# The second head's q and k as plain products, and new orders for the front, in a pre-norm attention and FFN kernel

## The chip, the cores and the metric

One Trainium2 chip, one core. The metric is the device time of one execution in microseconds (us). All inputs lie in the chip's memory when it starts and the output is written back to it.

## The reference

`x` is 1024 tokens by 512. Attention has 32 heads of width 128 (each head's q takes 192 columns of `wq`, of which the first 128 are used), then an FFN of three layers whose weights are signs.

```python
h = layernorm(x)
q = h @ wq  -> [S, 32, 192]; q = q[..., :128]
k, v = h @ wkv[:, :4096], h @ wkv[:, 4096:8192]   # [S, 32, 128] each
scores = q k^T / sqrt(192), causal mask, softmax over keys
x = x + (probs @ v) @ wo
h = layernorm(x)
x = x + ei(relu(ei(relu(s0 * h @ sign(k0)) * 2, k1, s1)) * 2, k2, s2)
```

`ei` multiplies the last fifth of its input by -4 before the product with +1 and -1 weights. The normalisations have no gain or bias.

## The kernel before, in words

Precision comes from pairs: every operand is held as a high and a low half (f16, or f32r for the output projection and the FFN), and a product is three matmuls, high by high, high by low, low by high. `xb` holds the normalised input, transposed, in blocks; `wqk` the halves of a head's q and k weights in slots A11, A12, S1 to S4 and A22.

**Heads.** From the second head on, q and k of a head come from seven products (steps `x1` to `x7`, `product`, L1138; six matmuls of 128x512 each). They are a Strassen-like scheme over 2 by 2 blocks: sums of weight blocks (`sums`, L508, on GpSimd), sums T1 to T4 of input blocks (`block_sum` and the split `sum_lo_part`, L872, on VectorE, with `sum_hi_part`, L646, on ScalarE), and gathers (`a2` to `a7`, `gather`, L878) that add the results into `qk32`. ScalarE and GpSimd split those into halves (`qk`). The first head has plain products instead (steps `y0` to `y3`, `plain_product`, L1150; twelve matmuls of 128x512 each), whose results go straight into `qkT`: high half on ScalarE (`plain_product_hi`, L657), low half on VectorE (L901). 

**Steps of a head.** `s0` to `s7` are scores of 128 queries against all earlier keys, into one of two PSUM buffers by turns; `m` the mask and maxima (VectorE), `e` the exponentials (ScalarE), `h` and `l` the high and low halves of the probabilities (ScalarE, VectorE, into four buffers of `p16`), `t` a transposing DMA of them (issued by SyncE). s(n) waits for l(n-2); h(n) waits for the t of four steps before, which frees its buffer. `v` projects values for a pair of heads, `pv` multiplies probabilities by values, `o` projects the output, with its addition on VectorE under the same name.

**Weights.** A head's q and k weights are loaded (`lqk`), their squares summed on ScalarE (`mx`), the 128 partial sums written to memory and read back spread over all partitions (`put`, `get`, both issued by SyncE; for the first weights a transpose on TensorE, `spread`, does this), a power-of-two scale is found (`sc`, `bounds`, VectorE), the weights scaled (`r`, ScalarE), and split on GpSimd (`wqk` for q, `wk` for the first head's k; `wv` for values, `wo` for the output).

**Order.** Each engine runs an order written out by hand for a group of two heads (L40 to L73), one string for the steady group and one for the front, in words such as `x3@2`: step x3 of the head that is 2 after the group's first. The front is group -1, so `@2` there is the first head, `@3` the second and `@4` the third. Groups -1, 0 and the last are written out in code and the rest is a loop (`groups`, L358). Each engine does its steps strictly in this order, SyncE too: a DMA behind a waiting one waits with it. The front also normalises the second half of the input (`stat`, `scale`, `root`, `apply`, `turn`, `nhi`, `nlo`, `keep`). Chains of matmuls use four PSUM banks; a chain waits until the one before it in its bank has been read (`bank_free`, L1120), in the front round robin, later by the string BANKS. `exists` (L95) drops what a head does not need; `wait` (L340) turns a head's count into a semaphore value.

Of the kernel before, what the change touches and what calls it, by code (L numbers as in the profile page):

```python
# [35 lines left out]

PLAIN = (Q0, K0, Q1, K1)
# [6 lines left out]
    spread2@2 y0@2 y1@2 turn4@2 turn5@2 turn6@2 turn7@2 v0@2 s0@2 v1@2 s1@2 v2@2 v3@2 y2@2 s2@2 y3@2 s3@2 x1@3 v4@2  # L44
    s4@2 x2@3 v5@2 s5@2 x3@3 v6@2 s6@2 v7@2 s7@2""", "")
# [23 lines left out]
    lqk0@4 lo0@2 t0@2 put0@4 get0@4 t1@2 t2@2 t3@2 t4@2""", "")  # L69
# [3 lines left out]
    wqk0@2 wk0@2 wv0@2 wv1@2 wqk0@3 sum0@3""", "")  # L73
# [21 lines left out]
def exists(g, step):  # L95

    h = GH * g + step[1]
    if h == 0 and (step[0] in ("x", "a", "snap", "sum", "qk", "mx", "sc", "r", "put", "get", "lqk", "lv") or step[0] == "wv" and step[2] == 2):
# [100 lines left out]
def build(nc, hidden, wq, wkv, wo, k0, s0, k1, s1, k2, s2, out):  # L199
# [21 lines left out]
    with ExitStack() as ctx:  # L221
# [118 lines left out]
        def wait(eng, s, g, per, j, n):  # L340

            if isinstance(g, int):
                if per * (GH * g + j) + n > 0:
                    eng.wait_ge(s, per * (GH * g + j) + n)
            else:
                assert per * (GH + j) + n > 0
                eng.wait_ge(s, g * (GH * per) + (per * j + n))

        def wait_pair(eng, s, g, per, j, n):

            if isinstance(g, int):
                if per * (g + j // GH) + n > 0:
                    eng.wait_ge(s, per * (g + j // GH) + n)
            else:
                assert per * (1 + j // GH) + n > 0
# [60 lines left out]
        def loading_step(q, g, step, j, n):  # L416

            if step == "lqk":
                wait(q, sum_lo, g, 3, j, -6)
                if isinstance(g, int) and GH * g + j == 2:  # L420
                    q.wait_ge(first_lo, 1)
                    q.wait_ge(plain_lo, 1)
                load_head(q, g * GH + j, j % 2)
            elif step == "lo":
                wait(q, wo_lo, g, 1, j, 0)
                load_out(q, g * GH + j)
            elif step == "lv":
                wait_pair(q, wv_lo, g, 3, j, -1)
                load_values(q, g + j // GH)
            elif step == "put":  # L430
                rows_to_dram(q, g, j, n)
            elif step == "get":
                rows_from_dram(q, g, j, n)

        @block.sync
        def _(sp):
# [15 lines left out]
            def sync_steps(g):  # L452
                for step, j, n in steps_of(SYNC_ORDERS, g):
                    if step == "t":
                        wait(sp, p_lo, g, 8, j, n + 1)
                        sp.sem_inc(turn_go, 1)
                        if isinstance(g, int) and GH * g + j == 1 and n == 0:
                            sp.wait_ge(t_lo, 4)


                        sp.dma_start_transpose(pT[:, j % 2, rows_of(n), :], p16[:, n % 4, 0:2 * (n + 1) * P]) \
                            .then_inc(turned[n % 4], 16)
                    else:
# [17 lines left out]
        def _(pool):  # L481
# [11 lines left out]
            def split_first(g, j):  # L493

                wait(pool, scaled[0], g, 1, j, 1)
                if isinstance(g, int) and GH * g + j == 1:
                    pool.wait_ge(plain_done, 3)
                wait(pool, done["x"], g, 7, j, -5 - 7)
                split(raw[:, j % 2 * 2, :], slots(HI, A11, 2), slots(LO, A11, 2), first_hi, first_lo,
                      lambda: wait(pool, first_hi, g, 1, j, 1), not (isinstance(g, int) and GH * g + j == 0))  # L500

            def split_plain():

                pool.wait_ge(plain_hi, 1)
                nc.gpsimd.tensor_tensor(slots(LO, S2, 2), raw[:, 1, :], slots(HI, S2, 2), ALU.subtract) \
                    .then_inc(plain_lo, 1)

            def sums(g, j):  # L508
# [17 lines left out]
                split(k, slots(HI, S1, 2), slots(LO, S1, 2), sum_hi, sum_lo,
                      lambda: wait(pool, sum_hi, g, 3, j, 2 - 3))
                wait(pool, sum_done, g, 4, j, 4 - 4)
                split(q, slots(HI, S3, 2), slots(LO, S3, 2), sum_hi, sum_lo,
                      lambda: wait(pool, sum_hi, g, 3, j, 3 - 3))  # L530

            def qk_lo(g, j, n):
                wait(pool, qk_hi_done[n], g, 1, j, 1)
                wait(pool, gathered[LAST[n]], g, 1, j, 0)
# [54 lines left out]
            def pool_steps(g):  # L589
                for step, j, n in steps_of(POOL_ORDERS, g):  # L590
                    if step == "wqk":
                        split_first(g, j)
                    elif step == "wk":
                        split_plain()
# [27 lines left out]
        def _(act):  # L622
# [29 lines left out]
            def keep_x1(g, j, bank):  # L652
                wait(act, done["x"], g, 7, j, 1 - 7)
                wait(act, gathered[3], g, 1, j, -1)
                nc.scalar.activation(x1[:, :], psC[:, bank, :], ACT.Copy, scale=OUT_DOWN).then_inc(x1_kept, 1)

            def plain_product_hi(n, bank):  # L657
                act.wait_ge(plain_done, n + 1)
                nc.scalar.activation(qkT[:, qk_slot(0, PLAIN[n]), HI, :], psC[:, bank, :], ACT.Copy, scale=OUT_DOWN) \
                    .then_inc(qk_hi_done[PLAIN[n]], 1)  # L660

# [144 lines left out]
        def _(dve):  # L806
# [17 lines left out]
            def norm_scale(b):  # L824
# [5 lines left out]
                dve.wait_ge(mv_done, 4 * b + 4)  # L830
                ve, root, inv, a, bb = (nrm[:, k, :] for k in range(5))
                nc.vector.tensor_scalar_add(ve, mv[:, first:first + 4, 1], EPS).then_inc(ve_done, 1)
# [45 lines left out]
            def gather(g, j, n, bank):  # L878

                wait(dve, done["x"], g, 7, j, n - 7)  # L880
                if n < 4:
                    wait(dve, x1_kept, g, 1, j, 0)
# [4 lines left out]
                for earlier in {4: (3,), 5: (4,), 6: (5,), 7: (5,)}.get(n, ()):  # L887
                    wait(dve, gathered[earlier], g, 1, j, 0)
# [12 lines left out]
            def plain_product_lo(n, bank):  # L901
                hi, lo = (qkT[:, qk_slot(0, PLAIN[n]), w, :] for w in (HI, LO))
                dve.wait_ge(qk_hi_done[PLAIN[n]], 1)
                nc.vector.scalar_tensor_tensor(lo, psC[:, bank, :], OUT_DOWN, hi, ALU.mult, ALU.subtract) \
                    .then_inc(qk_lo_done[PLAIN[n]], 1)
# [79 lines left out]
            def vector_step(g, step, j, n):  # L985
                if step == "stat":
                    norm_stats(n)
                elif step == "scale":
                    norm_scale(n)
                elif step == "apply":  # L990
# [33 lines left out]
            norm_scale(0)  # L1024
            for t in range(4):
# [29 lines left out]
            norm_scale(2)  # L1055
            for t in range(4):
# [7 lines left out]
            norm_scale(3)  # L1064
            ffn_lo(0)
# [20 lines left out]
        def _(pe):  # L1086
# [33 lines left out]
            def bank_free(g, before):  # L1120

                if before is None:
                    return
                kind, j, n = before
                if kind == "x":
                    wait(pe, x1_kept if n == 1 else gathered[n], g, 1, j, 0)
                elif kind == "y":
                    pe.wait_ge(qk_lo_done[PLAIN[n]], 1)
# [7 lines left out]
            def product(g, j, n, bank):  # L1136
# [4 lines left out]
                elif n == 3:  # L1141
                    wait(pe, sum_lo, g, 3, j, 0)
                if isinstance(g, int) and GH * g + j == 1 and b in T_USED:
# [6 lines left out]
            def plain_product(n, bank):  # L1150

                if n == 0:
                    pe.wait_ge(first_lo, 1)
                elif n == 1:
                    pe.wait_ge(plain_lo, 1)
                c, a = n // 2, (A11, S2)[n % 2]
# [27 lines left out]
            def project_v(g, j, n, bank):  # L1184

                if isinstance(g, int) and g + j // GH == 0:
                    if n == 0:
                        pe.wait_ge(bounded[0], 6)
# [41 lines left out]
            def tensor_step(g, step, j, n):  # L1230
# [6 lines left out]
                else:  # L1237
                    at = PLAN[(g if isinstance(g, int) else 1), step, j, n]
                    bank_free(g, at[1])
# [19 lines left out]
            spread(1)  # L1259
# [6 lines left out]
            def ffn_chain(k):  # L1266
# [10 lines left out]
                if before[0] != "ffn":  # L1277
                    bank_free(NG, before)
# [54 lines left out]
```

## Time and profile before

| | |
|---|---|
| median of 3 runs | 1162.95 us (1162.06 to 1163.11) |
| the profiled execution | 1162.55 us, span 1160.7 us |
| TensorE matmul busy | 1102.2 us, 95% |
| VectorE, ScalarE, GpSimd busy | 899.0, 678.8, 676.9 us |
| chain that ended last | TensorE 66%, VectorE 14%, issue 9%, ScalarE 6% |
| 40 to 90 us: mean granted clock in steps of 10 us | 1.00, 0.83, 0.66, 0.77, 0.72 |

The page has shares of the whole span; a timeline gives one engine's instructions with the idle time ahead of each and what ended it; a window gives busy time and granted clock of a stretch. PE is TensorE, PEld its weight loads, DVE VectorE, ACT ScalarE, POOL GpSimd, SPq SyncE's DMA issues. L numbers are lines of the kernel.

### The profile page before, as it was taken

The page shows a single profiled execution, that of the slowest core. Times are in us where ns is not written, and L with a number is a line of the kernel's source. Part 1 is how long each engine was busy: PE and PEld are TensorE (multiplying, and loading weights), DVE is VectorE, ACT ScalarE, POOL GpSimd, SP SyncE. Part 2 cuts the span into 40 slices and gives each one's busy share as a digit, 9 for nine tenths or more (in the row PEclk, how much of TensorE's full clock was granted, in tenths as well). Part 3 has the DMA queues.
Part 4 walks back from the last instruction along what each step waited for, and adds up shares of the span by engine and source line. Part 5 has one row for each costly group of instructions (what it writes and reads, how often), then busy time and mean ns, then how long its engine had stood idle before and what let it go on. Part 6 is the DMA issues. An engine that isn't in the chain of part 4 may idle for free.

```text
span 1160.7 us, 22159 instructions
## 1 busy us (share of the span) xinstructions
PE 1102.2 (95%) x6217; PEld 655.3 (56%) x6217; DVE 899.0 (77%) x1799; ACT 678.8 (58%) x1335; POOL 676.9 (58%) x694
## 2 busy tenths in 40 slices
PE   4859999999999999999999999999999999999898
PEld 2515555556565555556555555656565555656577
DVE  6658777887878777787878787787877787787873
ACT  6545665656565565666565565566665565655453
POOL 2417576675656667665657657665657757665300
PEclk9979999999999999999999999999999999999999
DMA  4055664545554553555554553555454554555601
GB/s 154 4 118 90 112 104 89 114 104 118 111 122 83 123 104 75 124 105 122 111 111 81 119 114 73 120 115 124 97 116 87 109 113 85 118 99 99 105 1 73
DMA packets 367511, 117.33 MB, mean 101 GB/s; under 512 B 313088, under 2 KB 361344, under 8 KB 367488
## 3 DMA queue, kind: packets, MB, share of 16 engines
q1 hardware_dynamic: 367488, 117.05, 48.1%
q8 instruction: 11, 0.18, 0.1%
q14 instruction: 12, 0.10, 0.0%
HBM read 39.39 MB, written 2.12 MB: 36 GB/s over the span
## 4 chain that ended last, share of the span: by engine, by line
PE 66%; DVE 14%; issue 9%; ACT 6%; POOL 3%; DMA 1%; DVEq 1%; ACTq 0%; SPq 0%; POOLq 0%
PE psC L1094 38%; PE psS L1094 14%; PE psC L1218 13%; DVE p L966 3%; DVE attn L949 2%; ACT attn L725 2%; DVE qk L899 2%; ACT raw L671 1%; DVE psS L959 1%; POOL wqk L488 1%; DVE res L982 1%; ACT psS L703 1%; POOL wqk L485 1%; DMA wmax_rows<-wmax 1%; DVE bound L921 1%
## 5 line engine op out<-in xcount | busy, mean ns | idle before, releaser
L1094 PE MATMUL psC<-xb,wqk 128*128 128x512 f16 x1350 | 331.9, 385 | 18.6 <-POOL wqk L488 8.0
L703 ACT ACTIVATE psS<-psS,negmax 128x128 f32<-128x128 f32 (+7 forms) x256 | 182.8, 714 | 238.1 <-DVE negmax L959 235.9
L1094 PE MATMUL psC<-wos,attn 128*128 128x512 f32 x768 | 254.3, 442 | 12.5 <-DVE attn L949 8.9
L959 DVE CUSTOM_DVE_ANT_0 psS<-psS,mask,undo_qk 128x128 f32<-128x128 f32 (+7 forms) x256 | 209.2, 822 | 67.9 <-PE psS L1094 50.8
L966 DVE SCALAR_TENSOR_TENSOR p<-psS,p 128x128 f16<-128x128 f32 (+7 forms) x256 | 193.0, 754 | 72.8 <-ACT p L711 69.8
L1094 PE MATMUL psS<-qkT 128*128 128x512 f16 (+3 forms) x1152 | 231.4, 328 | 6.9 <-DVE p L966 4.8
L1094 PEld LDWEIGHTS psC<-xb,wqk 128*128 128x128 f16 x1350 | 124.6, 99 | 169.9 <-issue 26.3
L982 DVE SCALAR_TENSOR_TENSOR res<-psC,rinv,res 128x512 f32<-128x512 f32 x256 | 190.4, 744 | 11.2 <-DVE rinv L973 6.9
L1218 PE MATMUL psC<-pT,v 128*128 128x512 f16 (+3 forms) x1152 | 197.6, 326 | 0.2 <-DMA pT<-p 0.2
L536 POOL TENSOR_TENSOR qkT<-qk,qkT 128x512 f16<-128x512 f32 x124 | 141.5, 1157 | 92.7 <-ACT qkT L696 89.6
L1094 PE MATMUL psC<-wvs,xb 128*128 128x256 f16 x1536 | 189.0, 273 | 0.5 <-issue 0.4
L711 ACT ACTIVATE p<-psS 128x128 f16<-128x128 f32 (+7 forms) x256 | 166.2, 649 | 20.4 <-DMA pT<-p 2.7
L485 POOL TENSOR_TENSOR wqk<-raw,one 128x512 f16<-128x512 f32 x124 | 115.7, 933 | 100.8 <-ACT raw L671 90.1
L1094 PEld LDWEIGHTS psC<-wos,attn 128*128 128x128 f32 x768 | 137.2, 190 | 63.3 <-DVE attn L949 16.1
L1094 PEld LDWEIGHTS psC<-wvs,xb 128*128 128x128 f16 x1536 | 147.3, 98 | 39.0 <-issue 12.5
L1218 PEld LDWEIGHTS psC<-pT,v 128*128 128x128 f16 x1152 | 108.8, 98 | 92.4 <-issue 5.2
L1094 PEld LDWEIGHTS psS<-qkT 128*128 128x128 f16 x1152 | 98.1, 98 | 109.5 <-issue 38.0
L488 POOL TENSOR_TENSOR wqk<-raw,wqk 128x512 f16<-128x512 f32 (+1 forms) x125 | 130.6, 1045 | 16.3 <-ACT wqk L690 6.5
L485 POOL TENSOR_TENSOR wvs<-raw,one 128x512 f16<-128x512 f32 x45 | 46.8, 1039 | 113.8 <-ACT raw L671 80.2
L899 DVE SCALAR_TENSOR_TENSOR qk<-psC,qk 128x512 f32<-128x512 f32 x124 | 98.8, 817 | 12.3 <-PE psC L1094 10.5
L696 ACT ACTIVATE qkT<-qk 128x512 f16<-128x512 f32 x124 | 75.9, 624 | 41.3 <-DVE qk L899 41.3
L717 ACT ACTIVATE v<-psC 128x256 f16<-128x256 f32 x128 | 48.7, 381 | 58.9 <-PE psC L1094 58.9
(90 smaller groups left out, 934.0 us busy)
## 6 DMA issues: line engine op xcount, KB each, us to landing
raw<-in_L_attn_wkv SPq DMA_DIRECT2D x64, 256.0 KB, 3.3
raw<-in_L_attn_wq SPq DMA_DIRECT2D x32, 256.0 KB, 3.4
raw<-in_L_attn_wo SPq DMA_DIRECT2D x32, 256.0 KB, 3.2
pT<-p SPq DMA_TRANSPOSE x256, 4.3
wrow<-wmax_rows SPq DMA_DIRECT2D x45, 64.0 KB, 4.6
res<-in_L_attn_hidden_states SPq DMA_DIRECT2D x8, 256.0 KB, 5.6
out<-res SPq DMA_DIRECT2D x8, 256.0 KB, 2.0
raw<-in_L_ffn_k SPq DMA_DIRECT2D x3, 256.0 KB, 3.9
```

Source lines behind the costliest of these rows:

```text
L485: nc.gpsimd.tensor_tensor(hi, src, one[:, :].to_broadcast([P, src.shape[1]]), ALU.mult) \
L488: nc.gpsimd.tensor_tensor(lo, src, hi, ALU.subtract).then_inc(lo_sem, 1)
L536: nc.gpsimd.tensor_tensor(lo, qk32[:, AT[n], :], hi, ALU.subtract) \
L696: nc.scalar.activation(qkT[:, qk_slot(j, n), HI, :], qk32[:, AT[n], :], ACT.Copy) \
L703: nc.scalar.activation(row, row, ACT.Exp, bias=negmax[:, n:n + 1], scale=-1.0, accum_out=rowsum[:, j % 2, n:n + 1]) \
L711: nc.scalar.activation(parts_of(n)[:, :, HI, :], psS[:, n % 2, 0:(n + 1) * P].rearrange("p (k s) -> p k s", s=P), ACT.Copy, scale=UP).then ...
L899: nc.vector.scalar_tensor_tensor(to, product, OUT_DOWN, base32, ALU.mult, ALU.add).then_inc(gathered[n], 1)
L959: nc.vector.tensor_tensor_reduce(row, row, mask[:, S - width:S], undo_qk[:, j % 2:j % 2 + 1], 3e38, ALU.add, ALU.min, negmax[:, n:n + 1]). ...
L966: nc.vector.scalar_tensor_tensor(parts[:, :, LO, :], psS[:, n % 2, 0:(n + 1) * P].rearrange("p (k s) -> p k s", s=P), UP, parts[:, :, HI, ...
L982: nc.vector.scalar_tensor_tensor(res[:, t, :], psC[:, bank, :], rinv[:, t:t + 1], res[:, t, :], ALU.mult, ALU.add).then_inc(added, 1)
L1094: last = nc.tensor.matmul(out_ap, w, x, start=k == 0, stop=k == len(terms) - 1)
L1218: last = nc.tensor.matmul(o, a, b, start=(kt == 0 and k == 0), stop=(kt == count - 1 and k == 2))
```

## The change

The second head's q and k are plain products too (`y4` to `y7`: q and k of tokens 0 to 511, then of 512 to 1023). Its q weights go to S3 and S4, its k weights to A11 and A12. Seven products, six gathers, GpSimd's sums and splits of that head are gone, and T1 to T4 are first read by the third head. All semaphore counts follow, a second group is written out ahead of the loop, `norm_scale` is cut in two with the part behind the square root in `norm_rest`, `spread1` moves behind `y0`, and the orders of the front are new on all five engines.

```diff
-    spread2@2 y0@2 y1@2 turn4@2 turn5@2 turn6@2 turn7@2 v0@2 s0@2 v1@2 s1@2 v2@2 v3@2 y2@2 s2@2 y3@2 s3@2 x1@3 v4@2
-    s4@2 x2@3 v5@2 s5@2 x3@3 v6@2 s6@2 v7@2 s7@2""", "")
+    y0@2 spread1@2 y1@2 spread2@2 turn4@2 turn5@2 turn6@2 turn7@2 v0@2 v1@2 v2@2 s0@2 s1@2 y2@2 s2@2 s3@2 y3@2 v3@2
+    s4@2 v4@2 s5@2 y4@2 v5@2 s6@2 y5@2 s7@2 y6@2 v6@2 y7@2 v7@2""", "")
...
-    nhi0@2 nhi1@2 mx1@2 nhi2@2 nhi3@2 mx0@3 keep0@2 keep1@2 keep2@2 keep3@2 r1@2 root1@2 r0@3 y0@2 vhi0@2 vhi1@2
-    y1@2 nhi4@2 nhi5@2 nhi6@2 nhi7@2 keep4@2 keep5@2 keep6@2 keep7@2 v0@2 e0@2 h0@2 v1@2 e1@2 h1@2 v2@2 v3@2 y2@2
-    e2@2 h2@2 y3@2 part0@2 e3@2 h3@2 mx0@4 part1@2 snap0@3 v4@2 e4@2 h4@2 v5@2 e5@2 h5@2 part2@2 v6@2 part3@2 e6@2
-    h6@2 v7@2 r0@4 e7@2 h7@2""", "")
+    nhi0@2 nhi1@2 nhi2@2 keep0@2 nhi3@2 mx0@3 keep1@2 keep2@2 mx1@2 keep3@2 root1@2 r1@2 vhi0@2 vhi1@2 nhi4@2 nhi5@2
+    y0@2 nhi6@2 keep4@2 keep5@2 nhi7@2 v0@2 keep6@2 y1@2 keep7@2 mx0@4 e0@2 h0@2 e1@2 h1@2 v1@2 v2@2 y2@2 e2@2 h2@2
+    e3@2 y3@2 r0@3 h3@2 part0@2 part1@2 e4@2 h4@2 v3@2 v4@2 e5@2 y4@2 h5@2 part2@2 part3@2 v5@2 y5@2 e6@2 h6@2 e7@2
+    h7@2 y6@2 r0@4 v6@2 y7@2 v7@2""", "")
...
-    nlo0@2 nlo1@2 nlo2@2 nlo3@2 sc1@2 sc0@3 stat4@2 stat5@2 stat6@2 stat7@2 scale1@2 apply4@2 apply5@2 apply6@2
-    apply7@2 y0@2 y1@2 nlo4@2 nlo5@2 nlo6@2 nlo7@2 v0@2 m0@2 sum0@2 l0@2 v1@2 m1@2 sum1@2 l1@2 v2@2 v3@2 y2@2 m2@2
-    l2@2 y3@2 part0@2 m3@2 l3@2 part1@2 v4@2 m4@2 l4@2 a2@3 sum2@2 v5@2 m5@2 l5@2 sum3@2 part2@2 v6@2 m6@2 l6@2
-    part3@2 a3@3 v7@2 m7@2 sc0@4 l7@2""", "")
+    nlo0@2 nlo1@2 nlo2@2 nlo3@2 stat4@2 stat5@2 stat6@2 stat7@2 scale1@2 sc1@2 rest1@2 apply4@2 apply5@2 apply6@2
+    apply7@2 nlo4@2 nlo5@2 sc0@3 nlo6@2 y0@2 nlo7@2 y1@2 v0@2 m0@2 m1@2 l0@2 sum0@2 l1@2 sum1@2 m2@2 m3@2 v1@2 l2@2
+    y2@2 v2@2 y3@2 sum2@2 l3@2 m4@2 part0@2 m5@2 l4@2 v3@2 sum3@2 v4@2 l5@2 m6@2 y4@2 part1@2 m7@2 v5@2 l6@2 sc0@4
+    y5@2 part2@2 l7@2 v6@2 y6@2 v7@2 part3@2 y7@2""", "")
...
-    lqk0@4 lo0@2 t0@2 put0@4 get0@4 t1@2 t2@2 t3@2 t4@2""", "")
+    lqk0@4 lo0@2 put0@4 t0@2 t1@2 get0@4 t2@2 t3@2 t4@2""", "")
...
-    wqk0@2 wk0@2 wv0@2 wv1@2 wqk0@3 sum0@3""", "")
+    wqk0@2 wk0@2 wv0@2 wv1@2 wqk0@3 wk0@3""", "")
...
+    if h <= 1 and step[0] in ("x", "a", "snap", "sum", "qk", "wqk"):
+        return False
...
             body(-1)
             body(0)
-            with eng.Fori(1, NG - 1) as g:
+            body(1)
+            with eng.Fori(2, NG - 1) as g:
...
-                wait(q, sum_lo, g, 3, j, -6)
-                if isinstance(g, int) and GH * g + j == 2:
-                    q.wait_ge(first_lo, 1)
-                    q.wait_ge(plain_lo, 1)
+                wait(q, sum_lo, g, 3, j, -9)
+                if isinstance(g, int) and GH * g + j in (2, 3):
+                    q.wait_ge(first_lo, GH * g + j - 1)
+                    q.wait_ge(plain_lo, GH * g + j - 1)
...
+                if isinstance(g, int) and GH * g + j == 2:
+                    pool.wait_ge(plain_done, 8)
+                wait(pool, done["x"], g, 7, j, -5 - 14)
+                to = S3 if isinstance(g, int) and GH * g + j == 1 else A11
+                split(raw[:, j % 2 * 2, :], slots(HI, to, 2), slots(LO, to, 2), first_hi, first_lo,
+                      lambda: wait(pool, first_hi, g, 1, j, 1), not (isinstance(g, int) and GH * g + j == 0))
+
+            def split_plain(h):
+
+                to = (S2, A11)[h]
+                if h == 1:
                     pool.wait_ge(plain_done, 3)
+                split(raw[:, 2 * h + 1, :], slots(HI, to, 2), slots(LO, to, 2), plain_hi, plain_lo,
+                      lambda: pool.wait_ge(plain_hi, h + 1), h == 1)
...
+            def norm_rest(b):
+
+                first = 4 * (b % NC)
                 ve, root, inv, a, bb = (nrm[:, k, :] for k in range(5))
-                nc.vector.tensor_scalar_add(ve, mv[:, first:first + 4, 1], EPS).then_inc(ve_done, 1)
                 dve.wait_ge(root_done, b + 1)
                 link(nc.vector.reciprocal(inv, root))
...
-            spread(1)
             groups(pe, tensor_steps)
```

## Rows read from the trace of the kernel before

**Rows 1.** The page: busy us, share of the span, instructions; then 40 slices.

```profile
PE 1102.2 (95%) x6217; PEld 655.3 (56%) x6217; DVE 899.0 (77%) x1799; ACT 678.8 (58%) x1335; POOL 676.9 (58%) x694
...
PE   4859999999999999999999999999999999999898
...
PEclk9979999999999999999999999999999999999999
```

**Rows 2.** Windows: length, then busy us of PE, PEld, DVE, ACT, POOL; clock; DMA.

```profile
43.00:79.00 36.00, 22.70 (x105) 10.93 (x103) 21.07 (x35) 17.41 (x30) 9.30 (x9) 0.81 0.38 81
...
43.00:86.20 43.20, 27.82 (x117) 12.57 (x115) 24.05 (x38) 19.96 (x35) 12.86 (x13) 0.76 0.38 79
...
110.00:210.00 100.00, 98.46 (x566) 57.57 (x565) 79.71 (x157) 60.03 (x121) 63.55 (x64) 1.00 0.59 111
300.00:400.00 100.00, 98.55 (x566) 57.58 (x565) 79.68 (x157) 59.39 (x118) 66.86 (x67) 1.00 0.48 102
```

**Rows 3.** Timeline of PE: start us, us, instruction, idle before it and its releaser.

```profile
31.43 0.33 PE L1094 MATMUL psS<-qkT 128*128 128x128 f16 x3 [1.84 <-ACT pT L642]
...
38.93 2.75 PE L1094 MATMUL psC<-xb,wqk 128*128 128x512 f16 x12
...
46.88 1.47 PE L1094 MATMUL psC<-wvs,xb 128*128 128x256 f16 x12
...
51.84 2.72 PE L1094 MATMUL psC<-xb,wqk 128*128 128x512 f16 x6 [2.51 <-issue]
...
63.11 2.74 PE L1094 MATMUL psS<-qkT 128*128 128x512 f16 x6 [4.57 <-DVE p L966]
...
72.16 4.33 PE L1094 MATMUL psC<-xb,wqk 128*128 128x512 f16 x12 [3.71 <-DVE v L943]
80.79 5.13 PE L1094 MATMUL psC<-xb,wqk 128*128 128x512 f16 x12 [4.30 <-DVE qk L899]
86.25 0.33 PE L1094 MATMUL psS<-qkT 128*128 128x128 f16 x3 [0.34 <-issue]
```

**Rows 4.** Timeline of SyncE's issues of DMAs.

```profile
48.26 0.35 SPq L406 DMA_DIRECT2D wmax_rows<-wmax  x1
55.80 0.33 SPq L413 DMA_DIRECT2D wrow<-wmax_rows  x1
56.24 6.04 SPq L461 DMA_TRANSPOSE pT<-p  x4
```

**Rows 5.** Timeline of ACT.

```profile
28.90 2.39 ACT L642 ACTIVATE pT<-psS 128x512 f32<-128x512 f32 x4 [0.55 <-DVE xb L859]
...
31.58 1.28 ACT L703 ACT_TABLE_LOAD   x1
...
47.09 1.05 ACT L685 ACTIVATE squares<-raw 128x1024 f16<-128x1024 f32 x1
...
61.25 0.81 ACT L711 ACTIVATE p<-psS 128x768 f16<-128x768 f32 x1 [2.67 <-DMA pT<-p]
...
74.10 1.15 ACT L671 ACTIVATE raw<-raw,bound 128x1024 f32<-128x1024 f32 x1 [4.91 <-DVE bound L929]
```

**Rows 6.** Timeline of DVE.

```profile
24.25 2.76 DVE L847 TENSOR_SCALAR xn<-res,mv,nrm 128x512 f32<-128x512 f32 x4
...
32.21 1.22 DVE L869 TENSOR_TENSOR xn<-pT 128x1024 f32<-128x1024 f32 x1
...
39.27 0.69 DVE L904 SCALAR_TENSOR_TENSOR qkT<-psC,qkT 128x512 f16<-128x512 f32 x1 [2.31 <-ACT qkT L659]
...
49.21 1.52 DVE L876 TENSOR_TENSOR xb<-xn,xb 128x1024 f16<-128x1024 f32 x1 [1.29 <-ACT xb L650]
...
64.10 1.22 DVE L876 TENSOR_TENSOR xb<-pT,xb 128x1024 f16<-128x1024 f32 x1
```

**Rows 7.** Timeline of POOL.

```profile
49.73 2.01 POOL L488 TENSOR_TENSOR wqk<-raw,wqk 128x512 f16<-128x512 f32 x1
...
79.17 1.04 POOL L485 TENSOR_TENSOR wqk<-raw,one 128x512 f16<-128x512 f32 x1
80.28 1.16 POOL L488 TENSOR_TENSOR wqk<-raw,wqk 128x512 f16<-128x512 f32 x1
```

More of the change, by code:

```diff
@@ L97, in exists @@
     h = GH * g + step[1]
-    if h == 0 and (step[0] in ("x", "a", "snap", "sum", "qk", "mx", "sc", "r", "put", "get", "lqk", "lv") or step[0] == "wv" and step[2] == 2):
+    if h <= 1 and step[0] in ("x", "a", "snap", "sum", "qk", "wqk"):
+        return False
+    if h == 0 and (step[0] in ("mx", "sc", "r", "put", "get", "lqk", "lv") or step[0] == "wv" and step[2] == 2):
         return False
@@ L345, in wait @@
             else:
-                assert per * (GH + j) + n > 0
+                assert per * (2 * GH + j) + n > 0
                 eng.wait_ge(s, g * (GH * per) + (per * j + n))
@@ L593, in pool_steps @@
                     elif step == "wk":
-                        split_plain()
+                        split_plain(j - 2)
                     elif step == "sum":
@@ L652, in keep_x1 @@
             def keep_x1(g, j, bank):
-                wait(act, done["x"], g, 7, j, 1 - 7)
-                wait(act, gathered[3], g, 1, j, -1)
+                wait(act, done["x"], g, 7, j, 1 - 14)
+                wait(act, gathered[3], g, 1, j, -2)
                 nc.scalar.activation(x1[:, :], psC[:, bank, :], ACT.Copy, scale=OUT_DOWN).then_inc(x1_kept, 1)
             def plain_product_hi(n, bank):
+                h, to = n // 4, PLAIN[n % 4]
                 act.wait_ge(plain_done, n + 1)
-                nc.scalar.activation(qkT[:, qk_slot(0, PLAIN[n]), HI, :], psC[:, bank, :], ACT.Copy, scale=OUT_DOWN) \
-                    .then_inc(qk_hi_done[PLAIN[n]], 1)
+                if h == 1 and to != K0:
+                    act.wait_ge(done["s"], 4 if to == Q0 else 8)
+                nc.scalar.activation(qkT[:, qk_slot(h, to), HI, :], psC[:, bank, :], ACT.Copy, scale=OUT_DOWN) \
+                    .then_inc(qk_hi_done[to], 1)
             def scale_weights(g, j, n):
@@ L692, in qk_hi @@
             def qk_hi(g, j, n):
-                wait(act, gathered[LAST[n]], g, 1, j, 0)
+                wait(act, gathered[LAST[n]], g, 1, j, -1)
                 wait(act, done["s"], g, 8, j, {Q0: -4, Q1: 0, K0: -8, K1: 0}[n])
@@ L878, in gather @@
             def gather(g, j, n, bank):
-                wait(dve, done["x"], g, 7, j, n - 7)
+                wait(dve, done["x"], g, 7, j, n - 14)
                 if n < 4:
-                    wait(dve, x1_kept, g, 1, j, 0)
+                    wait(dve, x1_kept, g, 1, j, -1)
                 reused = {2: Q0, 3: Q1, 4: K0, 5: K1}.get(n)
@@ L887, in gather @@
                 for earlier in {4: (3,), 5: (4,), 6: (5,), 7: (5,)}.get(n, ()):
-                    wait(dve, gathered[earlier], g, 1, j, 0)
+                    wait(dve, gathered[earlier], g, 1, j, -1)
                 product = psC[:, bank, :]
@@ L989, in vector_step @@
                     norm_scale(n)
+                elif step == "rest":
+                    norm_rest(n)
                 elif step == "apply":
@@ L1024, in _ @@
             norm_scale(0)
+            norm_rest(0)
             for t in range(4):
@@ L1055, in _ @@
             norm_scale(2)
+            norm_rest(2)
             for t in range(4):
@@ L1064, in _ @@
             norm_scale(3)
+            norm_rest(3)
             ffn_lo(0)
@@ L1118, in spread, with bank_free @@
                                     ident[:, :]).then_inc(spread_done, 1)
-            def bank_free(g, before):
+            def bank_free(g, bank, before):
                 if before is None:
+                    if bank == 3:
+                        pe.wait_ge(bounded[0], 6)
+                        pe.wait_ge(bounded[1], 1)
                     return
@@ L1125, in bank_free @@
                 if kind == "x":
-                    wait(pe, x1_kept if n == 1 else gathered[n], g, 1, j, 0)
+                    wait(pe, x1_kept if n == 1 else gathered[n], g, 1, j, -1)
                 elif kind == "y":
-                    pe.wait_ge(qk_lo_done[PLAIN[n]], 1)
+                    pe.wait_ge(qk_lo_done[PLAIN[n % 4]], 1 + n // 4)
                 elif kind == "v":
@@ L1141, in product @@
                 elif n == 3:
-                    wait(pe, sum_lo, g, 3, j, 0)
-                if isinstance(g, int) and GH * g + j == 1 and b in T_USED:
+                    wait(pe, sum_lo, g, 3, j, -3)
+                if isinstance(g, int) and GH * g + j == 2 and b in T_USED:
                     pe.wait_ge(t_lo, T_USED[b])
@@ L1150, in plain_product @@
             def plain_product(n, bank):
[L1152 to L1156, printed above, removed]
+                h, c, a = n // 4, n // 2 % 2, ((A11, S2), (S3, A11))[n // 4][n % 2]
+                pe.wait_ge(plain_lo if n % 2 else first_lo, h + 1)
                 pe.wait_ge(xt_lo, 4 * c + 4)
@@ L1277, in ffn_chain @@
                 if before[0] != "ffn":
-                    bank_free(NG, before)
+                    bank_free(NG, bank, before)
                 else:
```

47 lines of the change are left out of this document (19 added, 28 removed).

## The prediction

> **What bounds the kernel now.** I read the page's shares first [rows 1]. TensorE is busy for 1102.2 of 1160.7 us, at the full granted clock nearly everywhere; the two weak places are the first slices and the third, 58 to 87 us, which has 5 tenths busy and a clock of 7 tenths (so 1.2 GHz for part of it). The end of the kernel shows nothing comparable. The windows say the same with numbers [rows 2]: 100 us in the middle of the loop hold 98.55 us of matmul, 100 us that begin at 110 hold 98.46, and the 43.2 us from 43.0 hold only 27.82, at a mean clock of 0.76. From about 110 us on the kernel is matmul end to end, so whatever is won ahead of it comes out at the end one for one, unless the second group gives it back.
>
> So the place to read is TensorE's order of time there [rows 3]. The words of the orders are matched to it by shape: twelve 128x512 matmuls are one plain product y, six are one product x, twelve 128x256 are one v. Four waits stand out: 2.51, 4.57, 3.71 and 4.30 us, together 15.1. The work between them runs at half speed: six matmuls take 2.74 us, where twelve took 2.75 at 38.93. The other engines' rows name what each wait is for.
> - 2.51 us before x3 of head 1. It waits for every split of head 1's sums on GpSimd; the last, L488 at 49.73, takes 2.01 us [rows 7], to 51.74.
> - 4.57 us before s7 (63.11). s7 wants l5, that wants h5 on ScalarE, and h5 sat until 61.25 for a transposing DMA [rows 5]. SyncE issued four of those only at 56.24, behind get0@4, and this waited for put0@4 to land [rows 4]: the put was issued at 48.26 and the get at 55.80. The put in turn wanted the squares mx0@4 of 47.09 [rows 5]. A tiny DMA for a head that is two heads away holds up the transposes of head 0.
> - 3.71 and 4.30 us before x5 and x7 of head 1: their banks come free only through v7 and the gathers on VectorE, which stand behind l7 in its order, and l7 is late through the same delay, and on ScalarE r0@4 (74.10, after 4.91 us idle) stands ahead of e7 [rows 5].
>
> **The change part by part.** I take as mark the first scores of head 1, s0@1, at 86.25 [rows 3]. Beyond it both kernels issue the same steps in the same steady orders.
>
> *Work to the mark.* Prices at full clock, start to start: a y 2.6 us (38.93 to the next start 41.52; the row says 2.75), an x half of it, 1.3; a v 1.3 (46.88 to 48.19); s4 to s7 read 9984 columns, at 512 in 0.216 us 4.2 us. Before, from 42.17 where x1 of head 1 starts, there were x1 to x7, v4 to v7, s4 to s7 and x1 of the third head: 9.1 + 5.2 + 4.2 + 1.3 = 19.8 us of work. They took 86.25 - 42.17 = 44.1 us, so 24.3 us went to waits and to the half clock. After, from s4: four y, four v, s4 to s7 and x1 of the third head, 10.4 + 5.2 + 4.2 + 1.3 = 21.1. The second head's plain products thus cost 1.3 us (48 matmuls for 42).
>
> *What goes.* Nothing before the mark reads the sums of head 1, T1 to T4 or a gather. With the sums goes the 2.51 us; with the gathers and their banks go 3.71 and 4.30. put0@4 now stands ahead of t0, and mx0@4 ahead of e0, so the get waits beside t0 and t1 rather than in front of them; t1 is no longer behind it, and 4.57 goes too. With the four waits gone there should be no reason for the low clock.
>
> *What is late next, up to s4.* spread1 moves behind y0 and the reciprocal chain is split off as norm_rest, with sc1@2 between. y0 ends near 21.0, spread1 21.3, sc1@2 22.2, the rest 1.0 more, so the first apply is about 23.2 against 24.25 before; four applies take 2.76 [rows 6], and the turns and splits end about 0.7 us sooner. The last keep ends at 30.6 (before 28.90 + 2.39 = 31.3 [rows 5]). Behind it ScalarE now has mx0@4 (1.05) and the table load (1.28), both in [rows 5], then e0 and h0 (0.7): 33.7. VectorE: l0 0.3, sum0 1.15 (1.22 less overlap [rows 6]), l1 0.35, 35.5. TensorE has no filler there: s3 waits for l1, 0.65, then y3 2.6, to 38.8, v3 to 40.1. The halves of y3 (0.6 and 0.69 [rows 6]), with y2 and v2 ahead of it on VectorE, are ready at 40.5, and s4 starts then. All of y0 to y3, v0 to v3 and s0 to s3 is done at that point, which before was so at 42.17.
>
> *From s4 to the mark.* 19.8 us of TensorE's work before x1 bring v7's end to 60.3. I checked each want of it against the other queues: s5 wants l3 (42.2, reached at 42.6); y4 wants q of head 1 in S3, r0@3 to 40.9 and two GpSimd splits of 1.04 and 1.16 [rows 7], 43.3 against 43.6; y5 wants k, 45.6 against 48.7; s6 wants l4 (46.1 against 47.5); s7 wants l5 (48.8 against 51.3); y6 and y7 want banks freed long before. x1 of the third head wants A11, which y7 reads last: GpSimd's split starts at 59.1, while v7 still runs 1.3 us, and takes 2.25, so x1 waits 1.1 us. The mark would be 60.3 + 1.1 + 1.3 = 62.7.
>
> *Allowance.* VectorE held 21.07 us of work in 43 to 79 [rows 2]. After, it loses from this m3 and three gathers and gains y4 to y7 (0.69 each [rows 6]), about 21 us in the 22.2 us from 40.5: it has no slack, and TensorE and ScalarE each add small waits. The margins above are 0.3 and 0.4 us in two places. From 0 (all covered) to 9 us (every one of the five m, e, h, l rounds late by a split part or sum, about 1.8 each, 1.05 on ScalarE and 0.7 over the cover on VectorE); I take 1.5, near the lower end, since the later margins are 1.4 to 3 us. Mark at 64.2.
>
> *The port.* The L876 of 49.21 took 1.52 us while GpSimd worked, those of 64.10 took 1.22 with it idle [rows 6], and the L488 beside the first took 2.01 against 1.16 at 80.28 [rows 7]. After, part3 stands behind v7 on VectorE, at about 61, just where GpSimd makes the low half for x1. The Trainium skill (GPSIMD Engine Reference, Specifications) says that GpSimd shares its interfaces to SBUF with VectorE, in contention with instructions that have two SBUF inputs, which L876 has; the trace agrees. By it x1 would come up to 0.85 us later, and the sum be 0.85 worse. By the row at 80.28 nothing is added. The allowance holds either.
>
> *Smaller edits.* The second group leaves the loop: unrolled code at 110:210 is as dense as the loop at 300:400 [rows 2], so 0, within 0.5 us either way for an instruction fetch or a loop's start. Semaphore counts (-14, -9, 1-8 and so on) only follow two heads without sums: 0; the bank waits are the same kind. The later put1@0, get1@0 and wv0@2 keep their distance from the mark.
>
> Sum: 86.25 - 64.2 = 22.0 us less. The profiled execution took 1162.55 us (span 1160.7 and 1.85 around it), 0.4 under the median of 1162.95. 1162.55 - 22.0 = 1140.5 us.
>
> **Rivals.**
> *Half the gain.* One in-order queue falls behind: a 1.05-us part on ScalarE ahead of e4, e5 and e6 delays the round of scores, l and the next s. For it: VectorE has no slack, so a late l isn't made up. Against: y and v cover up to 3.9 us between scores. Five late rounds cost 9 us: 1149.5; three, 1146.
> *Slower, by the clock.* If the wait ahead of s3 and y3, about 1 us in my walk, grows to the 2.5 us of the row at 51.84, the clock falls there as it did in that row, and TensorE works from 36 us on at 1.2 GHz. y3, v3 and 21.1 us take double, 25 us more: 1165.5, slower than before. Against: the wait of 1.84 us before s0 of head 0 (31.43 [rows 3]) left the clock high, and my walk has half of that. It decides from about 2 us of wait on.
> *Given back.* The second group's own roundtrips (put1@0, get1@0) or GpSimd's sums of the third head set its start, and the mark moves without the rest: about 1161. Against: the puts follow mx1@2 at 62.8, as close to the mark as before, and the sums end at about 73 where x3 wants them at 81.
> *More than the sum.* The allowance isn't needed and the stall before the first o0 of head 0 shrinks: 1137.5.
>
> **How the numbers follow.** The sum 0.62; half the gain 0.22 (mostly 1144 to 1150); more than the sum 0.08; slower by the clock 0.04; given back 0.04. A run here can't tell under 0.2% (2.3 us) from nothing, so same is most of the given-back case, 0.03; slower 0.04; faster 0.93. The likeliest case alone spans 1137.5 to 1143.5. The range takes it, the allowance's far end and most of half the gain: 1136.5 to 1150.5.
>
> **What would show it.** In the profile after, s0 of head 1 near 64 us; one continuous stretch of matmul from about 36 us with a clock of 1.00 in 43 to 63; no transposing DMA waited for by ScalarE before 60 us; a wait of about 1 us ahead of the first x, ended by GpSimd; VectorE above 85% in 41 to 63; from 90 us on the same density as now. Wrong would be: waits over 2 us or a granted clock under 0.9 in 36 to 64; a first x past 67 us; or a difference in time that isn't the shift of the mark.

## The result and the profile after

The changed kernel takes 1141.78 us (median of 4 runs, 1140.5 to 1143.18) against 1162.97 for the kernel before on the same chip: 21.2 us less, ratio 0.982 with a 95% interval of 0.9803 to 0.9837. The forecast was 1140.5 us, with a range of 1136.5 to 1150.5. The profiled execution has a span of 1140.2 us, 20.5 less than before.

The lines of the page that answer to [rows 1]; the third slice is full and the clock high:

```profile
PE 1095.7 (96%) x6223; PEld 654.6 (57%) x6223; DVE 897.6 (79%) x1797; ACT 677.8 (59%) x1334; POOL 667.2 (59%) x682
...
PE   4989999999999999999999999999999999999998
...
PEclk9999999999999999999999999999999999999999
```

TensorE's timeline from s3 on answers to [rows 3] (columns as there). The mark, s0 of head 1, stands at 64.24. The four waits of together 15.1 us are gone. New are one of 1.26 us, as forecast ahead of the first x and ended by GpSimd, and smaller ones of 0.72 and 0.39 us ahead of s3 and s4:

```profile
36.44 0.82 PE L1113 MATMUL psS<-qkT 128*128 128x512 f16 x3 [0.72 <-DVE p L980]
37.09 2.75 PE L1113 MATMUL psC<-xb,wqk 128*128 128x512 f16 x12
39.68 1.47 PE L1113 MATMUL psC<-wvs,xb 128*128 128x256 f16 x12
41.55 0.97 PE L1113 MATMUL psS<-qkT 128*128 128x512 f16 x6 [0.39 <-issue]
...
60.22 1.47 PE L1113 MATMUL psC<-wvs,xb 128*128 128x256 f16 x12
62.95 1.46 PE L1113 MATMUL psC<-xb,wqk 128*128 128x512 f16 x6 [1.26 <-POOL wqk L492]
64.24 0.33 PE L1113 MATMUL psS<-qkT 128*128 128x128 f16 x3
```

The same stretch as windows (columns as in [rows 2]): clock 1.00, VectorE busy for 25.77 of 28 us.

```profile
36.00:64.00 28.00, 25.91 (x152) 14.55 (x153) 25.77 (x45) 22.11 (x40) 9.56 (x7) 1.00 0.64 123
```

SyncE's order, against [rows 4]: the put is issued at 32.53, t0 and t1 go out while it lands, and the get follows at 40.68.

```profile
32.53 0.34 SPq L410 DMA_DIRECT2D wmax_rows<-wmax  x1
35.02 2.64 SPq L465 DMA_TRANSPOSE pT<-p  x2
40.68 0.33 SPq L417 DMA_DIRECT2D wrow<-wmax_rows  x1
41.13 7.75 SPq L465 DMA_TRANSPOSE pT<-p  x3
```

86.25 - 64.24 = 22.0 us were won at the mark, but the spans differ by 20.5. The missing 1.5 us is lost behind it, evenly. The low half of attn, of which a head makes two, shows this by its first and last start, below in the kernel before and then in the changed one: they are 1015.0 us apart before and 1016.5 after. Read group by group in VectorE's timeline, from the first attn of one group of two heads to the first of the next, the distance is 65.75 us before and 65.88 after in every pass of the loop (within 0.02).

```profile
L949 DVE SCALAR_TENSOR_TENSOR attn<-psC,undo_v,attn x64: 742/751/752, 91.1 to 1106.1; 128x512 fp32r<-128x512 f32 x64
```

```profile
L963 DVE SCALAR_TENSOR_TENSOR attn<-psC,undo_v,attn x64: 741/750/752, 69.1 to 1085.6; 128x512 fp32r<-128x512 f32 x64
```

### The profile page after: what moved, and what is told of

Its sections match the earlier page's. It is cut to its first block, busy times and chain, and to the rows that moved or that the text cites. A ratio compares the mean times of both kernels' runs of the same rounds, so it can differ in the third digit from the quotient of the medians.

```text
span 1140.2 us, 21889 instructions
## 1 busy us (share of the span) xinstructions
PE 1095.7 (96%) x6223; PEld 654.6 (57%) x6223; DVE 897.6 (79%) x1797; ACT 677.8 (59%) x1334; POOL 667.2 (59%) x682
## 4 chain that ended last, share of the span: by engine, by line
PE 68%; DVE 13%; issue 9%; ACT 6%; POOL 3%; DVEq 1%; DMA 0%; ACTq 0%; POOLq 0%; SPq 0%
PE psC L1113 40%; PE psS L1113 14%; PE psC L1236 14%; DVE p L980 3%; DVE attn L963 2%; ACT attn L733 2%; DVE qk L912 2%; POOL wqk L492 2%; ACT raw L679 2%; POOL wqk L489 1%; DVE res L996 1%; DVE psS L973 1%; ACT psS L711 1%; DVE bound L935 1%; DVE negmax L973 0%
## 5 line engine op out<-in xcount | busy, mean ns | idle before, releaser
L1113 PE MATMUL psC<-xb,wqk 128*128 128x512 f16 x1356 | 328.1, 381 | 11.0 <-POOL wqk L492 9.4
L541 POOL TENSOR_TENSOR qkT<-qk,qkT 128x512 f16<-128x512 f32 x120 | 137.0, 1157 | 61.7 <-ACT qkT L704 61.7
L492 POOL TENSOR_TENSOR wqk<-raw,wqk 128x512 f16<-128x512 f32 x124 | 129.0, 1040 | 15.8 <-ACT wqk L698 6.3
L912 DVE SCALAR_TENSOR_TENSOR qk<-psC,qk 128x512 f32<-128x512 f32 x120 | 95.4, 815 | 10.0 <-PE psC L1113 8.4
L704 ACT ACTIVATE qkT<-qk 128x512 f16<-128x512 f32 x120 | 73.4, 624 | 37.9 <-DVE qk L912 37.9
```

The source lines that it names most:

```text
L492: nc.gpsimd.tensor_tensor(lo, src, hi, ALU.subtract).then_inc(lo_sem, 1)
L541: nc.gpsimd.tensor_tensor(lo, qk32[:, AT[n], :], hi, ALU.subtract) \
L704: nc.scalar.activation(qkT[:, qk_slot(j, n), HI, :], qk32[:, AT[n], :], ACT.Copy) \
L912: nc.vector.scalar_tensor_tensor(to, product, OUT_DOWN, base32, ALU.mult, ALU.add).then_inc(gathered[n], 1)
L1113: last = nc.tensor.matmul(out_ap, w, x, start=k == 0, stop=k == len(terms) - 1)
```

## The experiments

**The order of the put, three ways.** First the changed kernel with SyncE's old order and the squares back behind h3:

```diff
-    ... keep7@2 mx0@4 e0@2 h0@2 ... r0@3 h3@2 part0@2 ...
+    ... keep7@2 e0@2 h0@2 ... r0@3 h3@2 mx0@4 part0@2 ...
-    lqk0@4 lo0@2 put0@4 t0@2 t1@2 get0@4 t2@2 t3@2 t4@2
+    lqk0@4 lo0@2 t0@2 put0@4 get0@4 t1@2 t2@2 t3@2 t4@2
```

> The changed kernel with SyncE's old order of the front and the squares mx0@4 behind h3, where the kernel before had them about. Theory (the put's landing held up the transposing DMAs, and that was one of the four waits): put about 43.5, get and t1 about 51.5, h5 at 56 where it is at 48.2 now, TensorE idle 4 to 6 us ahead of s7, some of it at the half clock after: 5 to 9 us slower than the changed kernel, 1147 to 1151. Rival (the transposes only mattered because of the sums and gathers): at most 1.5 us slower.

Measured: 1149.23 us, ratio to the kernel before 0.9876 (0.9861 to 0.9891), 7.4 us slower than the changed kernel's 1141.78. The put goes out at 42.49 and holds everything until 50.12; s7 waits 6.10 us and then runs at half speed:

```profile
42.49 0.35 SPq L410 DMA_DIRECT2D wmax_rows<-wmax  x1
50.12 0.33 SPq L417 DMA_DIRECT2D wrow<-wmax_rows  x1
50.56 6.73 SPq L465 DMA_TRANSPOSE pT<-p  x4
```

```profile
58.12 2.74 PE L1113 MATMUL psS<-qkT 128*128 128x512 f16 x6 [6.10 <-DVE p L980]
60.65 4.13 PE L1113 MATMUL psC<-xb,wqk 128*128 128x512 f16 x12
```

Then SyncE's old order alone (only the last two lines of that diff).

> The changed kernel with SyncE's old order of the front alone; the squares stay ahead of e0. Theory: the put is issued at about 36.3 behind t0, lands at 44, t1 follows at 45 and lands at 49.3, one us after h5 wants it, which the cover of y5 takes up: 0 to 1 us slower, 1141.8 to 1142.8. If SyncE's order is what counts and not the place of the squares, it loses 4 us or more.

Measured: 1142.27 us (0.9815, 0.98 to 0.983), no difference beyond the noise. late_put differs from this run only in the place of the squares and takes 7.0 us more, so it is their place on ScalarE that counts; with them early, the put can stand on either side of t0. (Late squares under SyncE's new order were not run.) Last, these two moves in the kernel before, without the plain products and the change's other orders:

```diff
-    ... keep7@2 v0@2 e0@2 ... h3@2 mx0@4 part1@2 ...
+    ... keep7@2 v0@2 mx0@4 e0@2 ... h3@2 part1@2 ...
-    lqk0@4 lo0@2 t0@2 put0@4 get0@4 t1@2 t2@2 t3@2 t4@2
+    lqk0@4 lo0@2 put0@4 t0@2 t1@2 get0@4 t2@2 t3@2 t4@2
```

> The kernel before with two edits of the change alone: mx0@4 ahead of e0 on ScalarE, and SyncE's new order of the front. Theory (several waits, of which this removes the 4.57 us and shortens the next): 3 to 7 us faster than the kernel before, 1156 to 1160; the rest of the 21 us needs the sums and gathers gone. Rival (the orders alone bring most of it): under 1151.

Measured: 1158.26 us (0.9958, 0.9942 to 0.9973), 4.9 us faster than the 1163.18 beside it. The wait ahead of s7 falls to 2.35 us; those for the splits of the sums (2.63), v7 (1.13, 3.71) and the gathers (3.32) stay. Behind the first two of these waits the matmuls run at full speed, six of 128x512 in 1.46 and 1.47 us:

```profile
51.58 1.46 PE L1094 MATMUL psC<-xb,wqk 128*128 128x512 f16 x6 [2.63 <-issue]
59.14 1.47 PE L1094 MATMUL psS<-qkT 128*128 128x512 f16 x6 [2.35 <-DVE p L966]
```

The two moves alone bring 4.9 us of 21, and without the early squares the whole change brings 14, so the two parts nearly add up. The plain products under the old orders of the other engines were not run: how much of the 14 us is theirs, and how much is that of the orders on TensorE, ScalarE and VectorE, stays open.

**Who bounds the front.** Two additions to the changed kernel: y5's twelve matmuls made twice, and a spare subtraction on VectorE ahead of part0's:

```diff
+                if n == 5:
+                    chain(psC[:, bank, :], terms)
                 chain(psC[:, bank, :], terms).then_inc(plain_done, 1)
```

> The changed kernel with the twelve matmuls of y5 made twice (2.6 us more work for TensorE in the middle of the front, nothing more for VectorE). Theory (TensorE bounds the stretch from s4 to s0 of head 1, VectorE follows it closely): the full 2.6 us, 2.2 to 2.8 slower, about 1144.4, with s0 of head 1 at 66.9. Rival (VectorE's queue sets the pace, as the run with swapped slots suggests for the last steps): 0 to 1.3 us slower.

```diff
+                if m == 0:
+                    nc.vector.tensor_tensor(spare[:, :, :], src, xb[:, block, HI, :, :], ALU.subtract)
                 nc.vector.tensor_tensor(xb[:, block, LO, :, :], src, xb[:, block, HI, :, :], ALU.subtract).then_inc(t_lo, 1)
```

> The changed kernel with one more subtraction of 128x1024 on VectorE (1.2 to 1.9 us) ahead of part0's, into a spare buffer. Theory (TensorE bounds the middle of the front; VectorE waits 0.99 us there ahead of m7): most of it is taken up, 0 to 0.5 us slower. Rival (VectorE's queue sets the pace from l0 on): 1.2 us or more slower.

Measured: 1145.66 us (0.985, 0.9835 to 0.9866) and 1143.1 us (0.9834, 0.9819 to 0.9849) against the changed kernel's 1141.7 to 1141.8. That is 3.9 and 1.3 us more, both over what was expected (2.2 to 2.8, and 0 to 0.5), and the second is what its rival asked for (1.2 or more). These times also hold what differs from run to run at the start, where v0 came 1.16 and 0.27 us later than in the changed kernel's profile. Counted from v0, s0 of head 1 comes 38.81 us later with the matmuls (68.00 - 29.19), 37.01 with the subtraction (65.31 - 28.30) and 36.21 without either (64.24 - 28.03). So 2.6 of 2.6 us of matmuls come through. Of the subtraction it is 0.8 of 2.0 us: it took 1.90 us, part0's behind it took 2.06 us where it took 1.89 in the changed kernel, and m6 came 2.0 us later (19.66 us after v0, not 17.69).

```profile
44.16 1.90 DVE L891 TENSOR_TENSOR spare<-xn,xb 128x1024 f16<-128x1024 f32 x1
45.98 2.06 DVE L892 TENSOR_TENSOR xb<-xn,xb 128x1024 f16<-128x1024 f32 x1
```

TensorE bounds the stretch, and VectorE follows it with 1.2 us to spare where s6 waits for l4: the spare subtraction brings a wait of 0.63 us there.

**The 1.26 us ahead of the first x.** In the changed kernel, q of the second head in A11, k in S3, so that the third head's split need not wait for y7:

```diff
-                h, c, a = n // 4, n // 2 % 2, ((A11, S2), (S3, A11))[n // 4][n % 2]
+                h, c, a = n // 4, n // 2 % 2, ((A11, S2), (A11, S3))[n // 4][n % 2]
...
-                    pool.wait_ge(plain_done, 8)
+                    pool.wait_ge(plain_done, 7)
```

> Second head's q weights go to A11 and A12, its k weights to S3 and S4 (the changed kernel has it the other way round), so that the slots the third head's q needs are last read by y6 and not by y7. Theory (TensorE waits 1.26 us ahead of the first x only because GpSimd's split starts at y7's end): the split starts when r0@4 is done, about 59.3, ends at 61.6, the wait falls to about 0.1 and the time by 1.1 to 1.2 us against the changed kernel, to about 1140.6. Rival (VectorE, which ends y7's low half only at 64.5, sets the pace): s0 of head 1 comes sooner but what follows waits for VectorE, and the time stays at 1141.8.

Measured: 1143.27 us (0.9823, 0.981 to 0.9837), nothing won where 1.1 to 1.2 us was expected. The wait is gone, and s0 of head 1 comes 35.07 us after v0 and not 36.21, 1.1 us sooner. But VectorE is still at y7's low half, as the rival said, and head 1's first mask starts only at 65.21, when its scores have been ready since 64.3. The wait ahead of o0 of head 0 has grown from 1.69 to 2.38 us, and behind it the clock is at 0.57, where it was 1.00; the group of head 0 takes 66.16 us and not 64.82. Windows of 2 us (us, PE busy, clock) and TensorE's row:

```profile
70.00:72.00 2.00, 1.56 (x4) 0.57 0.00 0
72.00:74.00 2.00, 2.00 (x7) 0.57 0.00 0
```

```profile
70.44 1.62 PE L1115 MATMUL psC<-wos,attn 128*128 128x512 f32 x3 [2.38 <-DVE attn L965]
```

**The loop's 0.13 us.** Two runs: the kernel before with its second group written out, and the changed kernel with its semaphores raised at the start, so that all waits have their old constants. Of the second the first lines and one of the waits:

```diff
+            for s, count in [(done["x"], 7), (sum_done, 4), (sum_hi, 3), (sum_lo, 3), (x1_kept, 1)] + \
+                    [(s, 1) for s in gathered.values()]:
+                dve.sem_inc(s, count)
...
-                wait(dve, x1_kept, g, 1, j, -1)
+                wait(dve, x1_kept, g, 1, j, 0)
```

> The kernel before with its second group written out ahead of the loop, nothing else. Theory (the loop's code is what it was, writing out costs nothing): groups of 65.75 us from the second on, span within 1 us of 1160.7. Rival (a group written out, or the loop's later start, brings the 65.88): groups of 65.88 us and a span 1.5 us longer.

> The changed kernel with VectorE raising, at its start, the ten semaphores that two heads without sums leave behind (x_done by 7, sum_done by 4, sum_hi and sum_lo by 3, x1_kept and the gathered ones by 1), and all waits on them with the constants of the kernel before. Nothing else differs. In the profiles a group of two heads takes 65.88 us after and 65.75 before. Theory (the other constants make the loop need one more register instruction on GpSimd ahead of the value weights' split, with the wait for the scaled weights on it, so that this split starts 0.15 us after ScalarE and not 0.07): with the old constants the group is 65.75 us again and the time 1.3 to 1.7 us less than the changed kernel's, 1140.2 to 1140.5. Rival (the group's time hangs on where the front leaves the engines, or on the second group written out): 65.88 and no change.

Measured: the first, a single run of 1163.38 us, has groups of 65.77 us (65.85 for the written-out one alone) and a span of 1161.5; the second 1140.85 us (0.9813, 0.98 to 0.9826) and groups of 65.77 behind a written-out one of 65.83. Writing out thus costs 0.1 us once and 0.02 us in each pass. The constants cost the other 0.11 us in each of the 13 passes (65.88 against 65.77), and from the first to the last attn 1.7 us (1016.5 against 1014.8):

```profile
L963 DVE SCALAR_TENSOR_TENSOR attn<-psC,undo_v,attn x64: 742/751/752, 69.5 to 1084.3; 128x512 fp32r<-128x512 f32 x64
```

The whole time fell by 0.9 us, where 1.3 to 1.7 was expected, and by their intervals the two ratios can't be told apart; it is the groups, alike in every pass, that show the effect. What makes it is read from the program and the rows, not tested by itself. In the program's instructions, listed by engine, the loop of the changed kernel has a register instruction, `REGISTER_ALU`, that carries the wait for `scaled_v` ahead of the value weights' split on GpSimd, where the kernel before and the one with raised semaphores have the wait on the split itself. In the profiles ScalarE's scaling ends at the same time, 410.02 + 1.14 and 410.01 + 1.14, and GpSimd starts 0.07 us apart, first with the old constants, then with the new:

```profile
411.23 1.04 POOL L489 TENSOR_TENSOR wvs<-raw,one 128x512 f16<-128x512 f32 x1 [5.41 <-ACT raw L679]
```

```profile
411.30 1.04 POOL L489 TENSOR_TENSOR wvs<-raw,one 128x512 f16<-128x512 f32 x1 [5.53 <-ACT raw L679]
```

Four steps later VectorE's `undo_qk`, 128 numbers, lasts until GpSimd's instruction of that moment ends (415.93 + 1.03 in the changed kernel, where GpSimd's L541 ends at 416.95), and the l behind it starts with the delay. That accounts for 0.07 us of each pass; a second step of about 0.05 us comes at a2, where the list of the changed kernel also has one more instruction ahead of the work.

**The start, and a lean end of the front.** First the changed kernel once more. Then the kernel with raised semaphores (1140.85 us), which all further runs are built on, with TensorE kept busy ahead of y0:

> The changed kernel once more, as the reference on this chip for the two others. Its profile also tells what of its front varies from run to run: y0 and y1 took 5.34 us in the profile of the kernel before and 6.95 in that of the changed kernel, half of y0 at half speed. If that is by chance, this profile may have either; if the order (spread1 behind y0) brings it, it is again near 6.9. The loop's group is 65.88 us by the theory of the register instruction.

```diff
+            pe.wait_ge(first_hi, 1)
...
+            busy(7)       # seven matmuls of 128x384 into unused columns
             for t in range(4):
                 norm_transpose(t)
+            busy(5)
```

> The kernel with the semaphores raised at the start (1140.85 us), and TensorE kept busy ahead of y0: seven matmuls of 128x384 into unused columns ahead of the first transposes and five between the last of them and y0, 1.3 to 2 us in gaps of 3 and 1.6 us. Theory (y0 runs at half speed because TensorE did little ahead of it): y0 takes 2.6 to 3.2 us and not 4.2 to 4.8, spread1, sc1@2 and all behind them come 1.2 to 1.6 us sooner, about 1139.4. Rival (the half speed of y0 has another cause, or v0 waits for something else): no change, within 0.4 us.

Measured: 1141.72 us for the first (0.9822, 0.9809 to 0.9836), with y0 at 2.75 us: the half speed of y0 comes and goes. In the eight other profiles with spread1 behind y0 and no filler it took 4.15 to 4.76 us. With the filler 1139.86 us (0.9807, 0.9793 to 0.982), y0 at 2.75 us, and the five runs lie within 1.1 us, where those of the changed kernel spread over 2.1 to 2.7. That is 1.0 us under the raised semaphores alone, where 1.2 to 1.6 was expected, and the intervals of the ratios overlap; for the filler speaks y0, at 2.75 us in both profiles that have one and in only one of the nine that don't. Then the swap with part2 and part3 on GpSimd, without the filler:

```diff
-    ... y5@2 part2@2 l7@2 v6@2 y6@2 v7@2 part3@2 y7@2      (VectorE)
+    ... y5@2 l7@2 v6@2 y6@2 v7@2 y7@2
-    wqk0@2 wk0@2 wv0@2 wv1@2 wqk0@3 wk0@3                    (GpSimd)
+    wqk0@2 wk0@2 wv0@2 wv1@2 wqk0@3 wk0@3 part2@2 part3@2
```

> The kernel with the semaphores raised at the start, the swapped weight slots (no wait ahead of the first x), and the low halves of T1 and T4 (part2 and part3) made by GpSimd, which is idle from 48 to 60 us, and not by VectorE. Theory (with the slots swapped, VectorE's last steps of the front, part2, l7, part3 and the low half of y7, were what held the rest; the run with swapped slots alone gained nothing for that reason): VectorE is 2.4 us ahead, y7's low half is ready by 63, the first masks of head 1 start right behind its scores at about 63.3, and 1.0 to 1.4 us are gained over the same kernel without the two edits: about 1139.6. Rival (the port: the two subtractions on GpSimd hold VectorE up by as much as they relieve it): 0 to 0.4 us.

Measured: 1140.57 us (0.9807, 0.9794 to 0.982), 0.3 us under the raised semaphores alone, where 1.0 to 1.4 was expected. The first masks start right behind their scores, at 63.86, as the theory had it, but ScalarE is still at the squares mx0@3 and mx1@2 until 64.4, the wait ahead of o0 is 2.19 us and the clock falls again; the group of head 0 takes 65.98 us instead of 64.84. The rival's 0 to 0.4 us came, but the port that it blamed shows little: one subtraction on VectorE took 1.36 us and not 1.22. Last, both together, with nine matmuls ahead of o0 in its own free bank:

```diff
+                if isinstance(g, int) and GH * g + j == 0 and t == 0:
+                    for _ in range(9):
+                        nc.tensor.matmul(psC[:, bank, 0:3 * P], xb[:, B11, HI, 0, 0:P], xb[:, B11, HI, 0, 0:3 * P], start=True, stop=True)
```

> Raised semaphores, swapped weight slots, part2 and part3 on GpSimd, TensorE kept busy ahead of y0, and nine more matmuls of 128x384 (1.5 us) into the free bank of the first output projection o0, in the 2.19 us for which TensorE waits there once nothing holds up the first x. Theory (in the two runs with swapped slots the wait ahead of o0 grew from 1.69 to 2.2 and 2.4 us, the clock fell to 1.2 GHz for 3 to 4 us of work behind it, and that gave back what the swap had won): the clock stays at 1.00 over 68 to 76 us, the group of head 0 takes 64.9 us and not 66.0, and the time is 0.6 us under the kernel with the busy front alone (1139.86): about 1139.2. Rival (the loss behind o0 comes from the wait itself): 65.4 us or more for that group and 1139.9 or slower.

Measured: 1138.65 us (0.9787, 0.9774 to 0.98), 3.1 us under the changed kernel and the fastest here; 1139.2 was expected. From s0 of head 1 to o0 it is 6.26 us as in the run before, so nothing became ready sooner. Only the idle time is filled, the clock stays up, and the group takes 64.85 us. The 1.1 us lost there was thus the clock's:

```profile
65.65 1.63 PE L1254 MATMUL psC<-xb 128*128 128x384 f16 x9
68.00 0.94 PE L1124 MATMUL psC<-wos,attn 128*128 128x512 f32 x3 [0.72 <-DVE attn L971]
```

## Why the prediction was right

*The four waits.* All gone, and the clock is at 1.00, as forecast. late_put brings back the one behind the put and none of the others; before_early_put shows that the others stand without the plain products. That the plain products alone, under the old orders, would remove them was argued, not run.

*Up to s4: 40.5 forecast, 41.55 measured.* The step that failed is that the turns come 0.7 us sooner. y0 was priced at 2.6 us, from a profile of the kernel before in which y0 and y1 together took 5.34; it took 4.20, so spread1 came at 22.12 and not 21.0, and the turns at 24.93 against 24.85 before. One profile cannot show that this price is a matter of chance. It is one in both kernels: `again` has y0 at 2.75, and y0 with y1 took 7.03 us in before_early_put and 8.10 in before_unrolled. The wait for l1 ahead of s3 was foreseen as 1 us and was 0.72.

*From s4 to the mark: 22.2 forecast, 22.7 measured*, with the wait ahead of x at 1.26 for 1.1. The allowance of 1.5 us was used in full, 1.05 of it before s4. That the mark came to 64.24 for 64.2 is partly luck of two terms: y0 took up most of what was set aside for late queues.

*VectorE without slack*: its share was right, 92% in 36 to 64, where over 85% was forecast for 41 to 63. It had 1.2 us of slack all the same, as dve_more shows, near the 1.4 us of the walk's margin ahead of s6.

*The port.* The rule of the Trainium skill (GPSIMD Engine Reference, Specifications) held and the place was wrong. part3 started at 62.49, when the low half for x1 was nearly made (61.65 + 1.16, as in [rows 7]). The contention fell on the second head's splits, beside VectorE's sums and part0. q was ready at 44.72, only 0.1 us before y4 started, so that this margin was all but used up; k was ready at 47.93, 1.9 us before y5. In these rows an instruction that starts beside one of the other engine's is longer by nearly what that one still had to run: the sum of 41.37 ended at 42.58, 0.98 us after the first row's start, and this row is 0.84 us over its 1.04:

```profile
41.60 1.88 POOL L489 TENSOR_TENSOR wqk<-raw,one 128x512 f16<-128x512 f32 x1 [13.62 <-ACT raw L679]
43.56 1.16 POOL L492 TENSOR_TENSOR wqk<-raw,wqk 128x512 f16<-128x512 f32 x1
44.67 2.02 POOL L489 TENSOR_TENSOR wqk<-raw,one 128x512 f16<-128x512 f32 x1
```

*"Semaphore counts (...) only follow two heads without sums: 0".* Wrong: 0.11 us in each pass. With the written-out group, which was also put at 0 but with 0.5 us either way, this is the step that makes the forecast 1.3 us too low: 22.0 us at the mark, 20.5 at the end. By the prediction's own words a difference that isn't the shift of the mark would be wrong, and 1.5 us of it were.

*The rivals.* Half the gain did not happen, and given back only by these 1.5 us. The clock rival named a mechanism that later runs showed at another place, ahead of o0 and not of s3, where waits of 2.19 and 2.38 us lost the clock and 1.69 kept it. Its "from about 2 us of wait on" does not hold: in before_early_put the clock outlasted waits of 2.35 and 2.63 us, while 2.51 us in the same place as the latter lost it in the kernel before. The length of one wait alone does not decide.

## What to carry to other kernels

A roundtrip through memory for work two heads ahead belongs where its first step can't hold the queue: what counted here was when its producer ran, not the order of the queue behind it. A wait that is taken away on a tight path can move to the next in-order engine; look where it lands, since there it may cost the clock as well. And price no operation of the start from a single profile.

## What was not expected of the hardware

Changing constants in waits, with the same instructions of work, cost 0.11 us in every pass of the loop; the list of instructions has one more register instruction between a semaphore and its consumer there, and 0.07 us of the loss starts at it. y0 ran its first matmuls at 0.43 us each, half speed, in a stretch (18 to 22 us) whose granted clock is given as 1.00 in the profile after; in the lean kernel's profile the same stretch reads 0.62. In these profiles the durations, not the clock's row, tell the speed near the start:

```profile
18.09 4.20 PE L1113 MATMUL psC<-xb,wqk 128*128 128x512 f16 x12 [1.63 <-DVE xb L872]
```
